# The setup of a one-core two-layer kernel: first input loaded first, zeroing in two transfers behind the barrier, tables built behind the first norm

## The reference, cut to what matters

```
xn = layernorm(x)
x  = x + delta_rule_attention(xn) + two_layer_local_attention_net(xn)
xn = layernorm(x)
x  = x + latent_attention(xn) + mixture_of_6_experts_plus_shared(xn)
```

```
def _layernorm(x, axis=-1, eps=1e-05):
    m = jnp.mean(x, axis=axis, keepdims=True)
    v = jnp.var(x, axis=axis, keepdims=True)
    return (x - m) / jnp.sqrt(v + eps)
...
            q = q * cos * scale + rotate_half(q) * sin * scale
            k = k * cos / scale + rotate_half(k) * sin / scale
```

## Time and profile before

| | |
|---|---|
| median of 3 runs | 1885.97 us (1883.97 to 1886.47) |
| span of the profiled execution, first to last instruction | 1891.7 us |
| PE busy | 1692.1 us, 89% |
| DVE, ACT, POOL busy | 70%, 51%, 44% |
| mean granted clock of PE, share of full | 0.959 |
| moved by DMA | 100.56 MB, mean 53 GB/s |

### The profile page before, as it was taken

The page is one execution under the profiler, slowest core; times in us unless marked ns, Lnnn a source line. Parts: engine busy times, 40 slices in busy tenths (PEclk is TensorE's granted clock), DMA queues, the critical chain, the costliest instruction groups (busy, mean ns, idle before and its releaser), DMA issues. The chain is left out here.

```text
span 1891.7 us, 44267 instructions
## 1 busy us (share of the span) xinstructions
PE 1692.1 (89%) x16808; PEld 1123.2 (59%) x16808; DVE 1315.8 (70%) x3530; ACT 959.6 (51%) x2513; POOL 827.6 (44%) x827
## 2 busy tenths in 40 slices
PE   2698789998999999999999989999898999999787
PEld 1474557565775657656684657656575566755443
DVE  2654577767677778677777778687777778676373
ACT  1434544476345854467445754457534664456324
POOL 1725654554326444365436535265334554264000
PEclk9889989999799999999999999999989999999888
DMA  5220122201311023101222023200221013210020
GB/s 214 68 58 12 35 62 72 63 11 33 88 58 51 11 67 97 52 21 33 52 77 71 8 47 92 77 18 22 65 82 52 19 36 89 75 29 10 14 78 7
DMA packets 162147, 100.56 MB, mean 53 GB/s; under 512 B 59256, under 2 KB 149496, under 8 KB 161656
## 3 DMA queue, kind: packets, MB, share of 16 engines
q1 hardware_dynamic: 161648, 96.92, 19.2%
q10 hardware_dynamic: 288, 0.81, 0.2%
HBM read 55.36 MB, written 27.26 MB: 44 GB/s over the span
## 5 line engine op out<-in xcount | busy, mean ns | idle before, releaser
L1360 ACT ACTIVATE shared<-bank 128x512 f32<-128x512 f32 (+1 forms) x384 | 201.8, 532 | 205.9 <-PE bank L1067 203.6
L1834 POOL TENSOR_TENSOR soft<-soft,prec 128x512 f32<-128x512 f32 x128 | 132.5, 1041 | 371.8 <-DVE prec L1478 371.4
L1642 DVE TENSOR_REDUCE nmx<-bank 128x1 f32<-128x512 f32 (+3 forms) x352 | 222.9, 637 | 93.3 <-PE bank L1039 91.6
L1260 ACT ACTIVATE soft<-bank,nmax 128x128 f32<-128x128 f32 x512 | 180.2, 380 | 105.7 <-DVE nmax L1470 104.7
L1795 POOL TENSOR_TENSOR qk_rs<-qk_rs,minus_half 128x16 f32<-128x16 f32 x64 | 187.7, 2934 | 5.3
L718 PE MATMUL bank<-w_sb,hT 128*128 128x512 f32 x256 | 137.3, 627 | 5.6 <-DVE rot L1460 3.1
L1067 PE MATMUL bank<-shared 75*128 75x384 bf16 (+3 forms) x512 | 140.4, 302 | 0.0
L1066 PE MATMUL bank<-b_sb 128*128 128x128 bf16 x512 | 113.8, 224 | 25.6 <-ACT shared L1360 22.8
L1039 PE MATMUL bank<-shared 72*128 72x256 bf16 (+3 forms) x512 | 126.8, 300 | 0.0
L688 PE MATMUL bank<-c_sb,soft 128*128 128x128 f32 x608 | 98.6, 294 | 24.1 <-POOL soft L1834 18.1
L1066 PEld LDWEIGHTS bank<-b_sb 128*128 128x128 bf16 x512 | 48.9, 98 | 115.8 <-ACT shared L1360 70.3
(11 more groups left out here) (254 smaller groups left out, 4492.6 us busy)
## 6 DMA issues: line engine op xcount, KB each, us to landing
shared<-parts_dram SPq DMA_DIRECT2D x64, 288.0 KB
vm<-v_f SPq DMA_DIRECT2D x112, 128.0 KB, 2.4
parts_dram<-parts SPq DMA_DIRECT2D x96, 128.0 KB, 2.4
L_dram<-the SPq DMA_DIRECT2D x32, 256.0 KB, 2.3
shared<-Z_dram SPq DMA_DIRECT2D x32, 256.0 KB, 3.5
shared<-L_dram SPq DMA_DIRECT2D x32, 256.0 KB, 4.4
shared<-X_dram SPq DMA_DIRECT2D x32, 256.0 KB, 4.9
w_sb<-weights SPq DMA_DIRECT2D x1, 4167.0 KB, 19.7
```

The costliest lines, as they stand in the source:

```text
L1260: a = af(v4(p_sb, 2, 4)[:, j, g], place("fS", j)[:, g * P:(g + 1) * P], ACT.Exp, bias=nmax[:, at:at + 1], accum_out=psums[:, at:at + 1])
L1360: af(v4(PTm, 2, GROUP)[:, u % 2, i, 0:n], place("mST", b, i)[:, 0:n], ACT.Exp).then_inc(mexp_done, 1)
L1642: reduce(v3(nmx[:], HM)[:, h:h + len(heads), c], v3(place("mS", b, t)[:, 0:len(heads) * (c + 1) * P], len(heads)), AX, ALU.max, negate=Tru ...
L1834: tt(p, p, spread(prec[:, at:at + NPAIR], P), ALU.mult).then_inc(fnorm_done, 1)
```

## The change

- SP's first transfer is now the first sequence of `x`; it counts on a new semaphore `x_first`, and so does `consts_bf`, which ACT still issues first.
- The rests of weights and constants and the zeroing are issued behind the barrier, at the start of SP's part of the main block. The zeroing is two transfers, one for each DRAM tensor, each of 128 partitions x 8 pieces x 258 elements, instead of eight.
- The setup block has no part for DVE any more, and no engine waits in it for a transfer. POOL's clearing is unchanged.
- DVE's cast of `consts_bf` stands ahead of the first statistics, behind a wait for `x_first`. The eight tables and `norm_w` stand behind the first `happly`, behind a wait for `setup_loads`.
- PE waits for `setup_loads` before its first transposes. `x_load` of the first sequence does nothing; `x_loaded` counts from the second on.
- The semaphore `ft1_done`, and POOL's wait for it in `fqk`, are gone: `frot_done`, which POOL waits for too, is set by a later instruction of the same engine.

```diff
             @block.sync
             def _(sp):
+                sp.dma_start(v3(cols(x_tm, 0, T), NT), x[0:1].rearrange("a (t p) d -> p (a t) d", p=P)).then_inc(x_first, 16)
                 sp.dma_start(c_sb[:, 0:early_c], consts[:, 0:early_c]).then_inc(setup_loads, 16)
                 sp.dma_start(w_sb[:, 0:early_w], weights[:, 0:early_w]).then_inc(setup_loads, 16)
-                sp.dma_start(w_sb[:, early_w:], weights[:, early_w:]).then_inc(late_loads, 16)
-                sp.dma_start(c_sb[:, early_c:], consts[:, early_c:]).then_inc(late_loads, 16)
-                sp.wait_ge(zeroed, 2)
-                for c in range(NT):
-                    sp.dma_start(in_dram(X_dram, c), v3(zeros, H0)).then_inc(dram_zeroed, 16)
-                    sp.dma_start(in_dram(Z_dram, c), v3(zeros, H0)).then_inc(dram_zeroed, 16)
-                sp.wait_ge(setup_loads, 16 * 3)
 
             @block.scalar
             def _(act):
-                act.dma_start(shared[:, 0:B_N], consts_bf).then_inc(table_load, 16)
+                act.dma_start(shared[:, 0:B_N], consts_bf).then_inc(x_first, 16)
                 act.dma_start(r_sb[:], rows.to_broadcast([P, R_N])).then_inc(setup_loads, 16)
...
                     if b:
                         pe.wait_ge(fqT_copied, ch(b - 1, 1, 0))
+                    else:
+                        pe.wait_ge(setup_loads, 48)
                     transposes(place("hT"), lambda i: v3(hn_tm, NT)[:, i]).then_inc(head_psum, 1)
...
                         if m == 0:
-                            act.wait_ge(dram_zeroed, 32 * NT)
+                            act.wait_ge(dram_zeroed, 32)
...
+                def tables():
+                    dve.wait_ge(setup_loads, 48)
+                    for l in range(DEPTH):
+                        for cos, sin, row, c_out, s_out in (("qcos", "qsin", "qs", "qc", "qs"), ("kcos", "ksin", "ks", "kc", "ks")):
+                            g = R(row)[:, l * DF:(l + 1) * DF]
+                            tt(v3(tab[c_out][l], NT), v3(C(cos), NT), repeat(g, NT), ALU.mult)
+                            m = tt(v3(tab[s_out][l], NT), v3(C(sin), NT), repeat(g, NT), ALU.mult)
+                    link(m)
+                    ts(v3(norm_w[:], H0), repeat(R("norm_w"), H0), -0.5 * DV ** 0.5, None, ALU.mult)
+
                 def hln(b):
-                    dve.wait_ge(x_loaded, 16 * (b + 1))
                     if b:
+                        dve.wait_ge(x_loaded, 16 * b)
                         dve.wait_ge(head_norm_done, b)
+                    else:
+                        dve.wait_ge(x_first, 32)
+                        nc.vector.tensor_copy(b_sb[:], shared[:, 0:B_N])
                     moments("h", v3(cols(x_tm, b % 2, T), NT), head_asked)
...
                     apply("h", v3(hn_tm, NT), v3(cols(x_tm, b % 2, T), NT), head_root, b + 1, head_norm_done)
+                    if b == 0:
+                        tables()
...
-                    pool.wait_ge(ft1_done, m + 1)
                     pool.wait_ge(frot_done, m + 1)
...
             @block.sync
             def _(sp):
+                sp.dma_start(w_sb[:, early_w:], weights[:, early_w:]).then_inc(late_loads, 16)
+                sp.dma_start(c_sb[:, early_c:], consts[:, early_c:]).then_inc(late_loads, 16)
+                wide = NT * H0 * HEAD_ROOM // (8 * P)
+                for m in (X_dram, Z_dram):
+                    sp.dma_start(m.rearrange("(p a b) -> p a b", a=8, b=wide), repeat(zeros[:, 0:wide], 8)).then_inc(dram_zeroed, 16)
 
                 def x_load(b):
+                    if b == 0:
+                        return
...
                     if b == 0:
-                        sp.wait_ge(dram_zeroed, 32 * NT)
+                        sp.wait_ge(dram_zeroed, 32)
```

More of the change, by code:

```diff
@@ L416, in latent_tiles @@
             return v3(place("lat", b)[:, 0:NT * (LAT + NE)], NT)
+        x_first = ctx.enter_context(nc.semaphore("x_first"))
         late_loads = ctx.enter_context(nc.semaphore("late_loads"))
@@ L443, in build @@
         fss_done = semaphore("fss_done")
-        ft1_done = semaphore("ft1_done")
         frot_done = semaphore("frot_done")
@@ L582, in build @@
         assert numbers == list(range(numbers[0], numbers[0] + len(numbers)))
-        table_load, zeroed, tables_done = x_loaded, head_root, head_norm_done
+        zeroed = head_root
         early_w, early_c = W_AT["wo0"][0], C_AT["rcos"][0]
@@ L614, in _ @@
                 pool.wait_ge(zeroed, 7)
[L616 to L633, removed]
         nc.sync.sem_clear(range(numbers[0], numbers[-1] + 1))
@@ L1457, in fqk @@
                     ps = v3(place(("fq", "fk")[i], c)[:], HF)
-                    tt(v3(cols(dst, n % 2, T), HF), ps, repeat(cols(tab[tc][l], c, DF), HF), ALU.mult).then_inc(ft1_done, 1)
+                    tt(v3(cols(dst, n % 2, T), HF), ps, repeat(cols(tab[tc][l], c, DF), HF), ALU.mult)
                     dve.wait_ge(fss_done, m + 1)
```

## The result

| | before | changed |
|---|---|---|
| median at the time of the prediction | 1886.22 us (1883.97 to 1888.43, 4 runs) | 1864.14 us (1859.08 to 1868.28, 4 runs) |
| ratio to before | | 0.990, 95% interval 0.9865 to 0.9935 |
| profiled execution: span, mean granted clock | 1891.7 us, 0.959 | 1866.3 us, 0.960 |

The forecast was 1865.1 us in a range of 1861 to 1869.5. A second and a third set of the same kernel, run later, gave medians of 1856.8 and 1859.8 us (ratios 0.9878, 0.9817 to 0.9938, and 0.9858, 0.9821 to 0.9895). One of the 59 later runs of the kernel before, 1905.9 us at a mean granted clock of 0.949, was in a slower state than all others and is left out of every comparison.

A forecast was written before the change was run, and what follows sets the result against it. The prediction took PE, 89% busy in fixed order, as bound, with an uncovered idle head until 33.49 us; starting PE at 12.55 gains 20.9 us, other terms 0, so 1885.97 - 20.9 = 1865.1 us, range 1861 to 1869.5.

The forecast's parts named there:

- SP's stay in the setup: Setup block: without SP's zeroing, POOL's clearing ends it at 3.84 us, and the main block starts at about 4.9.
- The norm path: First sequence on DVE and POOL: inputs in at 7.6 us, cast 0.76 and norm 3.93, normed input at 12.3.
- The weights' path: First loads: `setup_loads` full at 12.50 us, 0.76 of it for `x`, so PE starts at 12.55 instead of 33.49.
- Tables at 15.4: DVE behind the first norm: tables done at 15.4 us, cost 0 with 3 us of cover, 2.9 without it.
- Late loads: Late weights and constants, issued at 4.9 us: all in at 22.3, first used by PE at 50.9, cost 0.
- Zeroing near 28.5: Zeroing behind the loads: 2.11 MB at 345 GB/s take 6.1 us; first softmax at 43.3, 12 us or more of cover.
- Control flow under traffic: All engines enter the main block at 4.9 us with the DMA engines full: claimed to cost nothing more.
- rival 2: Main block's start: engines' code comes late under full DMA engines, PE at 20.1 us, gain 13.4, 1872.6 us; chance 4%.
- Clock: PE's start: at 1.2 GHz, reaching 2.4 GHz some 7 us later, as before; taken as 0, 2 us kept for the range.
- Rival 1: PE's start: the norm path sets it, at 14.8 us, gain 18.7, 1867.3 us; chance 14%.
- Rival 3: ACT's first softmax: slow scattered zeroing becomes the bound, 6.5 us lost, 1892.5 us; chance 2%.
- Rival 4: Later in the kernel: something tied to the launch swallows the gain, 1886 us, no change; chance 2%.

The follow-up runs named there:

- x7: The changed kernel with the zeroing in 64-byte pieces instead of 1032-byte ones: median 1882.0 us, ratio 0.9981 to the kernel before.
- x2: The changed kernel with the load of `x` third on SP's queue, behind the first parts of `c_sb` and `w_sb`: median 1867.6 us.
- x3: The changed kernel with DVE's tables ahead of the cast and the first norm, behind their wait for `setup_loads`: median 1867.1 us.
- x10: The kernel before with only the semaphore `ft1_done` and POOL's waits for it removed: median 1888.3 us, ratio 1.0016.

## Why the prediction was right

By its own steps:

- *SP's stay in the setup, main block at 4.9:* 4.82. The barrier's 1.1 us held.
- *The norm path, ready at 12.3:* 10.2. `x` and `consts_bf` were in at 5.68, not 7.6. I had let the 256 KB of `x` delay `consts_bf`, from its old landing at 6.8; in fact it landed sooner with `x` at the head of the other queue: 4.2 us after its issue in x7, where `x` is first, against 5.9 in x2, where `x` is third (6.1 before). `c_sb` itself took 6.1 us to land in x2 and 8.3 in the changed kernel. Whether the 512-byte pieces of `x` are the reason was not tried. It is an error of 2.1 us which cost nothing, because the other path decided; the margin of 0.25 us between the paths was in fact 2.7.
- *The weights' path, 12.50:* 12.9 (1.77 + 11.1). `x` cost 1.2 us of it and not 0.76. The term for PE's start was 20.9 us and measured 20.5.
- *Tables at 15.4, 3 us of cover:* done at 15.96, DVE then idle for 3.29. Their price without cover, 2.9, is borne out by x3 less x2, 2.8 us.
- *Late loads all in at 22.3:* the weights landed at 4.82 + 17.8 = 22.6, the constants behind them 18.8 us after their issue at 5.20, at 24.0.
- *Zeroing near 28.5, at 345 GB/s or faster:* 32.7, at 235. I had taken the longer pieces to be no slower than the old ones, and they were slower; 10 us of cover were left of the 12.
- *`ft1_done`: 0:* x10, none. `x_first` takes its place, so the number of semaphores stays the same.
- *Control flow under traffic:* the first instructions of ACT and SP behind the barrier come 1.0 us after POOL's last clearing (4.82 against 3.83), while the loads are running. The rule of the Trainium skill ("Runtime: NRT & Kernel Launch", Instruction fetch mechanics) on the fetch behind a taken branch, which rival 2 priced at 7 us, cost nothing visible here. Rival 2 is out.
- *Clock:* I kept 2 us. The start's clock gave about 0.4 us in the first profile and 1.0 in the second. But over the whole run the clock goes with a spread of 29 us in the kernel before and of 23 us in the changed one (1849.8 to 1872.9), which no term of mine contained; I had taken 1.3 us each way from three runs. So the mechanism and the size of the gain were right by their steps, but that the median of four runs came out 1.0 us from the forecast, and inside the range, was luck: the next sets of the changed kernel gave 8.3 and 5.3 us less, below the range. My base of 1885.97 was itself 3.7 us above the median of the 58 later runs.
- *Sum:* 20.9 forecast; at equal clock 1881.9 - 1861.1 = 20.8 +- 1.0.

Rival 1 did not come about; x2 shows its mechanism, a norm path that sets the start, but only with `x` third in the queue. Rival 3 needed pieces of 64 bytes (x7), and then reached no change, not a loss. Rival 4 is excluded by the shift of 21.05 us at the first use of the late weights and by the 20.8 us at the end.

## What to carry to other kernels

In this program, whose engines follow fixed orders, time at the head counted in full: 20.5 us at PE's first instruction were 20.8 +- 1.0 at the end. In such a program, read from PE's first instruction back, list each thing it needs with its landing time, and then let only that thing be waited for, in the order in which the queue delivers it. Freeing SP from the zeroing was a third of the gain here; the rest needed a setup without waits, the input first in the queue, and the work that needs only the input ahead of the work that needs more. Before comparing variants that differ by less than 1%, look at the granted clock of each run: a stretch with the same instructions was 6.8 us longer in one execution than in another, and a fit with the clock narrowed a standard deviation of 6.6 us to 1.6. But first see whether the variant itself moved the clock, as x7 did: then the comparison at equal clock leaves out a part of its cost.

## What was not expected of the hardware

- The mean granted clock of one and the same kernel before lay between 0.953 and 0.972, and the time went with it by 1.46 us for each 0.001. What decides whether PE falls to the lower level in a stretch such as 450 to 510 us was not tried.
- Zeroing in pieces, written from SBUF to DRAM: 1032 bytes at multiples of 1032: 235 GB/s; 1024 at multiples of 1024: 381; 512: 346; 64: 89.
- A transfer's issue can hold its engine: 13.75 us for the second zeroing, 12.08 us for a transfer of 128 KB behind 64-byte pieces (x7). What stands behind it on that engine's list, with no tie to either, is late with it.
